# Moving the second query tile, the combine transposes, the first bias product and the last input load in a hand-ordered attention and expert kernel

## The reference

```
q, k, v = (x @ W.T + b) for each of q, k, v;  q, k = rope(q), rope(k)
out = softmax(q k^T / 4) v;  x = x + out @ Wo.T + bo
combine = sum over the two best experts of one_hot * softmax(top two logits)
out = xc + sum_e combine_e * (act_e @ w2_e.T + b2_e)
```

## Time and profile before

| | |
|---|---|
| median of 3 runs | 1063.61 us |
| profiled execution: its own time | 1064.35 us |
| its span, first to last instruction | 1062.5 us |
| mean granted TensorE clock | 0.961 of full speed |
| TensorE matmuls busy | 935.2 us (88%) |
| DVE busy | 765.6 us (72%) |
| ScalarE busy | 750.6 us (71%) |
| GpSimd busy | 406.1 us (38%) |
| mean share of the DMA engines' time | about 42% |
| windows 0 to 7, from first exponential to first exponential | 85.7, 121.3, 121.2, 127.1, 119.8, 120.8, 100.5, 102.8 us |
| before the first window, after the last | 65.9, 97.5 us |

### The profile page before, as it was taken

How to read it: one execution, slowest core, us unless ns; L and a number is a source line. 1 busy time by engine, 2 the same in 40 slices (tenths; PEclk the granted TensorE clock), 3 DMA queues, 4 the chain that set the end, 5 groups by cost and what they waited for, 6 DMA issues and landing times. The chain is left out here.

```text
span 1062.5 us, 16544 instructions
## 1 busy us (share of the span) xinstructions
PE 935.2 (88%) x5217; PEld 398.7 (38%) x5288; DVE 765.6 (72%) x1514; ACT 750.6 (71%) x1018; POOL 406.1 (38%) x341
## 2 busy tenths in 40 slices
PE   5669898999988999989989999889998999998496
PEld 3312222244332444334342444334442444344364
DVE  5851202689858886679858888688867786779797
ACT  1458895867867687767768677787878887885252
POOL 3525205352365325534263533652332324143310
PEclk9869998999999999989999999999999999999699
DMA  5264473325535343445534245344544453513121
GB/s 170 89 160 105 96 142 83 86 81 131 126 66 142 96 113 98 108 106 131 124 72 115 81 111 131 87 119 120 116 100 99 114 127 85 117 52 104 35 61 35
DMA packets 79984, 109.76 MB, mean 103 GB/s; under 512 B 22530, under 2 KB 56722, under 8 KB 76818
## 3 DMA queue, kind: packets, MB, share of 16 engines
q1 hardware_dynamic: 61460, 83.47, 33.4%
q10 hardware_dynamic: 18432, 25.17, 8.3%
HBM read 82.90 MB, written 25.69 MB: 102 GB/s over the span
## 5 line engine op out<-in xcount | busy, mean ns | idle before, releaser
L877 ACT ACTIVATE probs<-S 128x1024 f32<-128x1024 f32 x512 | 513.0, 1024 | 144.4 <-PE S L726 143.0
L726 PE MATMUL S<-Qs,Ks 98*128 98x512 bf16 x1024 | 301.8, 388 | 21.4 <-ACT probs L877 18.2
L740 PE MATMUL OP<-probs,V 128*17 128x512 f32 x2048 | 275.5, 610 | 3.6 <-ACT O L886 3.6
L964 POOL TENSOR_TENSOR act_lo<-act_sb,act_hi 128x512 fp32r<-128x512 f32 x112 | 152.5, 1363 | 134.0 <-ACT act_hi L866 133.7
L726 PEld LDWEIGHTS S<-Qs,Ks 98*128 98x128 bf16 x1024 | 79.4, 99 | 200.6 <-ACT probs L877 97.6
L712 PE MATMUL D<-W,act_hi 128*128 128x256 f32 x448 | 130.7, 324 | 13.4 <-DVE acc L1183 3.6
L1183 DVE SCALAR_TENSOR_TENSOR acc<-D,combh,acc 128x256 f32<-128x256 f32 x224 | 97.3, 475 | 55.0 <-PE D L712 54.6
L958 POOL TENSOR_SCALAR W<-W2b 128x512 fp32r<-128x512 bf16 x64 | 41.5, 649 | 222.4 <-PE D L712 177.2
L1191 DVE SCALAR_TENSOR_TENSOR th_sb<-th_sb,g_sb 128x512 f32<-128x512 f32 x112 | 107.3, 958 | 14.4 <-ACT th_sb L853 10.7
L712 PE MATMUL D<-W,act_lo 128*128 128x256 f32 x448 | 112.1, 282 | 0.0
L712 PEld LDWEIGHTS D<-W,act_hi 128*128 128x128 f32 x448 | 85.1, 190 | 39.2 <-DVE nsq L1045 6.8
(11 more groups left out here) (172 smaller groups left out, 1014.4 us busy)
## 6 DMA issues: line engine op xcount, KB each, us to landing
W<-in_w ACTq DMA_DIRECT2D x64, 256.0 KB, 2.8
Ks<-k_scr SPq DMA_DIRECT2D x32, 384.0 KB
W2b<-in_w ACTq DMA_DIRECT2D x64, 128.0 KB, 2.9
Ks<-k_scr SPq DMA_DIRECT2D x32, 256.0 KB
o_scr<-O SPq DMA_DIRECT2D x32, 256.0 KB, 4.7
Qs<-q_scr SPq DMA_DIRECT2D x32, 192.0 KB
k_scr<-parts SPq DMA_DIRECT2D x12, 384.0 KB, 3.3
q_scr<-parts SPq DMA_DIRECT2D x12, 384.0 KB, 3.4
```

Of the source, the lines that this page charges most:

```text
L726: last = mm(S[:, j2, C * i:C * (i + 1)], Ks[0:SROWS + MROWS, g % 2, j, P * kt:P * (kt + 1)], Qs[0:SROWS + MROWS, g % 2, j, :], start=True, ...
L740: last = mm(OP[32 * j:32 * j + VW, :], V[:, kt, HG * g + j, :], probs[:, s % 2, C * j:C * (j + 1)], start=kt == 0, stop=kt == KT - 1)
L877: nc.scalar.activation(probs[:, s % 2, 2 * C * j2:2 * C * (j2 + 1)], S[:, j2, :], ACT.Exp, scale=SCALE).then_inc(exp_done, 1)
L964: tt(act_lo[:, e % 2, it, :], act_sb[:, a % 2, :], act_hi[:, e % 2, it, :].bitcast(FP32), ALU.subtract).then_inc(lo_s, 1)
```

## The change

- `combT` goes from half-step 32 to 31, `b20` from 33 to 32; `b21` stays at 34.
- `part1` of every tile comes 4 half-steps after its product, not 3 (the first bf16 part and the square on ScalarE).
- `qk1` goes from 12 to 20 in windows 1 to 5, with its whole chain: rotation 22, first part 24, length 25, second part 27, third part 30.
- For the last chunk, `x1_in` and `x1_b` are issued in half-steps 43 and 55 of the last window, and no longer in half-steps 0 and 11 behind it.
- In the part behind the last window the reciprocal of the last sums is issued in step 2, place 1, and no longer in step 3, place 0. In the windows it stays in step 3.

```diff
-    AT = {"stats1": 43, "rstd1": 45, "xn": 49, "x_next": 50, "xT0": 54, "xT1": 55, "qk0": 10, "qk1": 12, "qk2": 22,
-          "qk3": 30, "rope": 2, "part1": 3, "length": 5, "part2": 7, "part3": 10, "v0": 37, "v1": 42, "gmax": 1,
+    AT = {"stats1": 43, "rstd1": 45, "xn": 49, "x_next": 50, "xT0": 54, "xT1": 55, "qk0": 10, "qk1": 20, "qk2": 22,
+          "qk3": 30, "rope": 2, "part1": 4, "length": 5, "part2": 7, "part3": 10, "v0": 37, "v1": 42, "gmax": 1,
...
-          "combT": 32, "b20": 33, "b21": 34}
+          "combT": 31, "b20": 32, "b21": 34}
...
+    LAST_IN, POST_END = {}, {k: [e for e in l if e[0] not in ("x1_in", "x1_b")] for k, l in POST.items()}
+    for st, h in (("x1_in", 43), ("x1_b", 55)):
+        place(LAST_IN, h, (st, 0))
...
             if post:
-                todo += [(st, a, before) for st, a in POST.get((step, place), [])]
+                todo += [(st, a, before) for st, a in (POST_END if b is B else POST).get((step, place), [])]
                 todo += [(st, a, before) for st, a in EXPERTS.get((step, place), [])]
+            if b is B - 1 and n == NCH - 1:
+                todo += [(st, a, (b, n)) for st, a in LAST_IN.get((step, place), [])]
...
-                    if kt == 3 and not first and place in (None, 0):
+                    if (kt, place) in ((3, None), (2, 1)) and not first:
                         dve.wait_ge(sum_r, 64 * (G + 1))
                         v.reciprocal(rec_c[:, :], sums_c[:, :]).then_inc(rec_s, 1)
```

## The result

The changed kernel took 1075.87 us (median of 4 runs, 1074.45 to 1078.82), the kernel before 1065.4 beside it (4 runs, 1063.59 to 1067.9): ratio 1.010, 95% interval 1.0064 to 1.0136. The forecast was 1049, its range 1043 to 1060. The profiled execution took 1074.53 (span 1072.7), 10.2 us more than the 1064.35 of the profiled one before.

What follows compares the result with a forecast made beforehand. TensorE was taken to bound the windows except where it stops. Terms -0.4 -1.2 -1.3 -1.2 -3.3 -9.3 +1.5 = -15.2 us against the profiled 1064.35 gave 1049, range 1043 to 1060.

Steps and rivals of the forecast that it cites:

- the rule: VectorE instructions with two SBUF inputs and GpSimd ones reading SBUF exclude each other; half-step 22's norm could be 1 us late.
- the sum: All forecast terms added: -15.2 us against the profiled 1064.35, with nothing for the norm or for SyncE's later transfer.
- Rival B: Half-step 24 worse than counted, from blocked DVE pairs and later logits, and the clock falls as before: 1074 us; chance 0.07.
- knot at 24: Copy of nfT, length product, its reduction, logits and gates' chain follow one another at half-step 24, DVE being full.
- Part 1: Transposes to 31, first bias product to 32: the 1.65 us stop at the second bias product goes; -0.4 us, clock apart.
- rival A: TensorE's stop only moves, ahead of the length product of half-step 35, and the clock falls as before: 1057 to 1059; chance 0.22.
- The size 9.3: Gain in us if the 1.2 GHz clock level at half-step 35 stays away in windows 1 to 4.
- Part 2: Second tile from half-step 12 to 20, first parts later: 2.9 us earlier at 22, mostly lost at 24; -1.2 in four windows.
- Windows 0 and 1: First two attention loops: -1.2 us in window 0 from later first parts; -1.3 in window 1, 3.8 gained and 2.5 lost.
- Tail: Behind the last window: earlier reciprocal, and DVE's sums no longer waiting for GpSimd's bias sum; -3.3 us.
- Windows 6 and 7: Last two attention loops, without preparation: 0.2 us gained each from the earlier transposes and bias product, -0.4 together.

Runs made afterwards that it cites:

- experiment 1: Changed kernel with GpSimd's rotation of the second tile cut to 8 of 512 columns in windows 0 to 5 (keys wrong); 1060.74 us, one run.
- experiment 2: Changed kernel with SyncE's transfer of the second tile's parts issued in half-step 32, not 30; 1071.03 us, one run.
- experiment 5: Kernel before with only the second tile moved to half-step 20; 1074.18 us, one run.
- experiment 3: Changed kernel with both the second tile's rotation cut to 8 columns and its transfer at half-step 32, the latter from window 1 on; 1052.65 us, one run.
- experiment 4: Changed kernel with the second tile back at half-step 12, all else as changed; 1053.85 us (median of 5), ratio to before 0.9899.
- experiment 7: Kernel before with only the combine transposes at half-step 31 and the first bias product at 32; 1061.1 us (median of 10), ratio 0.9963.
- experiment 8: Kernel before with only the last x and its bias sum taken into window 7 and the tail's reciprocal half a step earlier; 1064.35 us, one run.
- experiment 6: Changed kernel with the reciprocal put back half a step, which alters only the part behind the last window; 1081.19 us, one run.
- experiment 10: Kernel of experiment 4 with the sum of x and bias issued as four GpSimd instructions in every window; 1054.37 us (median of 4), ratio to before 0.9887.

## Why the prediction was wrong

- **The step that failed first** is in the paragraph on the rule: "By the rule the norm could be 1 us late in each window; ScalarE's new 1.24 us covers it, so the sum takes nothing." The rule was right, its use was not. I blocked one DVE instruction; the norm is four, and three met a GpSimd instruction, so it was 3.04 us longer. The cover was a different engine's 1.24 us, too short and partly in series: ScalarE's copy of the transposes waited 1.70 us, and the exponential behind it waits in order. With the low clock that followed it cost 13.9 us in five windows, where the sum had nothing (experiment 1). The Trainium skill (SBUF — State Buffer, section Who interferes with whom) calls the port pair that the two engines share an exclusive lock. The rows of 1.48 us beside GpSimd's 1.43 agree, and the lesson is to charge it per instruction.
- **The second** is "The DMAs of the second tile's parts leave SP's queue at 30, not 22 ... Nothing waits." I asked who needs these parts and not who stands behind them on SyncE. Seven loads did, and behind those the output's store; 10 to 12 us (experiment 2), where the sum had nothing. With the move alone it cost nothing (experiment 5).
- **Rival B had the right place and side** (knot at 24, 1074 us against 1074.53 measured) but by another mechanism: blocked DVE pairs, later logits and a clock that still falls at 35. I gave it 0.07. Experiments 1 and 3 show the cause; B's number was right partly by accident, since its clock loss did not happen.
- **Part 1 was right in mechanism**: the stop of 1.65 at the second bias product is gone (the first one stops 0.99 instead, forecast 0.5), the clock at 35 stays up in all five windows, TensorE stops 1.07 us ahead of the length product (forecast 1.4 to 1.6; 1.32 in experiments 4 and 7) and holds its clock, so rival A fell. The size 9.3 was met partly by luck: experiment 4 gives 9.4, but with transposes and product alone it is 5.9 (experiment 7), since I had charged nothing for the half-steps behind, and the later first parts, of which I had expected nothing there, bring the other 3.5. And the 9.3 came from one execution: in experiment 8 half-step 35 of windows 2 and 3 took 3.1 us less with the same program.
- **Part 2 up to half-step 22**: -2.9 forecast, -2.95 measured. Half-step 24 grows to 2.85 us by ScalarE's new work, without the rotation (experiment 1), and 25 shrinks by as much. In windows 2 to 5 the move without its two meetings gives -0.8 (experiment 3 against 4) where -1.2 was forecast.
- **Windows 0 and 1**: window 0 -1.95 against -1.2. In window 1 the forecast for the move was 3.8 gained and 2.5 lost; experiment 3 against 4 has 2.5 gained and 2.5 lost.
- **Tail**: -2.6 against -3.3. The output product began and lasted as forecast; DVE's second sum came 0.8 us later than I took it. The bias sum in window 7, "at most one blocked DVE instruction, 1 us", blocked one for 2.05 us: here a blocked instruction cost about what its neighbour, 2.80 us long, had left, not what another pair had cost. Windows 6 and 7, +1.3 where I had -0.4, are mostly this.

## What to carry to other kernels

Before moving a stage to another slot, list for each engine and each DMA queue what stands behind it there, and for each resource that excludes (a port pair, a PSUM bank) what runs in that slot: here both later places tried for one chain met something that the old one did not. Charge a port conflict per instruction met and with the neighbour's full length, and split a long GpSimd instruction where a short DVE one on the critical path must get in between. Time one edit alone before bundling: here a bundle of five edits held a gain of 1% (experiment 4) and a loss of 2%. And before testing an edit make sure that it changes the program where the question is asked; experiment 6 didn't.

## What the runs showed that I had not expected

- Four DVE instructions of 0.48 us grew to 1.5 in three of the four cases, beside GpSimd instructions of 1.26 to 1.44: in the rows the two engines alternate, one whole instruction each.
- GpSimd's sum of 128x1024 beside DVE's instruction took 2.80 us in one instruction and 3.71 in four, and let DVE in after one piece: 1.10 instead of 2.74. In window 2 four pieces took 2.79 us and one instruction 2.82.
- A store issued behind seven loads on SyncE held up the fetch that follows it for 7.3 us instead of 3.8.
- A stop of 1.65 us had the clock at 0.5 right behind it in windows 1 to 4 before and not in window 5; one of 3.06 in windows 3 to 5 after and not in window 2, but in window 2 as well in the second execution (experiment 6); one of 1.32 in one of five windows of experiment 10 and in none of experiment 4. So the same stop in the same program may or may not lower the clock.
